# Cross attention with K made by seven products of halves and read back from DRAM, in place of scores from the context itself

## The chip, the core and the metric

One NeuronCore of a Trainium2 chip runs the whole program. The metric is the device time of one execution in microseconds (us), as a median of several runs. The engines are TensorE (PE; its weight loads are PEld), VectorE (DVE), ScalarE (ACT), GpSimd (POOL) and SyncE (SP), which here only issues DMAs.

## What is computed

The program is a small perceiver of two layers over x (8 batches of 64 tokens, width 512) with a context of 8 x 1601 rows of width 1024. The change lies in the cross attention of the second layer:

```python
B, N, DIM = (8, 2048, 512)
M, CTX = (128, 1024)
HEADS, DH = (16, 64)
...
q = _split_heads(jnp.einsum('bnd,df->bnf', x, Wq))
kv = jnp.einsum('bmc,cf->bmf', context, Wkv)
k, v = jnp.split(kv, 2, axis=-1)
...
k = jnp.concatenate((nk, k), axis=-2)
v = jnp.concatenate((nv, v), axis=-2)
q = q * scale
sim = jnp.einsum('bhid,bhjd->bhij', q, k)
attn = jax.nn.softmax(sim, axis=-1)
out = jnp.einsum('bhij,bhjd->bhid', attn, v)
```

All of it is f32. The kernel gets f32 accuracy from f16 products: a number is kept as a high half and a low half (what the high half leaves), and a product is the sum of three: high by high, high by low, low by high. So every operand is "split": ScalarE writes the high half, VectorE the low one (raw minus high).

## The kernel before

The program is a row of stages, each with its own instruction streams for the five engines and a barrier at its end; semaphores order the engines within a stage.

Through the first stages (names dp_, mi_, ms_, mo_, bn_ and cq_) TensorE also makes V = context x Wv (names vw_, class `ValueWork`) between the stages' own products, and writes it to DRAM (`vd`). The last 34 context tiles of V are made in stage cq by `QuadWork`, 17 quads. A quad takes two context tiles and both halves of the contraction and of the features, and makes the four blocks of the result by seven products of halves (Strassen's scheme in Winograd's form) instead of eight; GpSimd makes the sums of context blocks and splits four of the seven operands, VectorE splits three, ScalarE makes high halves, and VectorE adds the products up (line 677, `cq_held`) and splits the results (line 691, `vw_vst`). The products rotate over six PSUM banks.

Stage ca (`attend`) takes a step f for each of 64 pairs of heads (8 batches by 8 pairs; f = 8 b + p). It never makes K. In step f, `project` multiplies the K weights of the pair by the queries, laid out block-diagonally in `ca_q_diag` by GpSimd (24 products of 128 columns, lines 1820 to 1822), to the query in context space `ca_qw` (split by lines 1911 and 1964). `chunk` multiplies that by the context of the batch, `CUTS = [0, 448, 896, 1249, KEYS]`, with KEYS = 1602 (the null key is the last): 4 chunks x 8 parts of the contraction x 3, 96 products (lines 1841 to 1843). The context of the next batch is loaded tile by tile (`ca_stage`) and split (lines 1905, 1957) into a ring of three half batches. Then the softmax: VectorE takes the maxima of the two halves of the scores (line 1969) and the bias (1973), ScalarE the exponentials with their sums (1919), VectorE the reciprocal (1978, 1981), ScalarE the weights' high half (1928), VectorE the low half (1986). SP transposes both halves by DMA (`ca_turned`, line 1769), and two steps later `attend_to` multiplies them by V, which SP has loaded from `vd` (`ca_vals`). After four pairs VectorE copies the results out (`leave`, lines 1995 and 1997). The order on TensorE is written out:

```python
for f in range(NF + 2):
    if f < NF:
        chunk(f, 0)
    if f + 1 < NF:
        project(f + 1, 0)
    if f < NF:
        chunk(f, 1)
    if f >= 2:
        attend_to(f - 2)
```

and likewise on the other engines; each engine takes its instructions strictly in that order. During V's quads, the first half batch of the context is loaded and split for stage ca (`first_high`, `first_low`), and in the stage before eight K-weight items ("keyw") are split. After ca follows stage co (`project_out`).

## Time and profile before

| | |
|---|---|
| median of 3 runs | 3063.41 us (3062.07 to 3064.23) |
| the profiled execution | 3065.92 us, of which the span from first to last instruction is 3063.9 us |
| busy: TensorE, weight loads | 2838.0 us (93%), 1507.4 us (49%) |
| busy: VectorE, ScalarE, GpSimd | 1625.4 us (53%), 1041.0 us (34%), 248.5 us (8%) |
| mean granted TensorE clock | 0.967 of full |
| DMA | 343.00 MB, mean 112 GB/s; SP's queue 40.8% of 16 engines' span |

The busy time of an engine is the time in which at least one of its instructions ran. TensorE's products overlap, so the duration of one is longer than its distance to the next. Shares over the whole span are a mean over stages with different limits, which is why the rows below are from stretches of it.

### The profile page before, as it was taken

To read this page: it belongs to the slowest core of one execution; us is meant where nothing else is said; L and a number is where in the kernel's file an instruction comes from. 1 tells how busy PE (TensorE), PEld (TensorE's weight loads), DVE (VectorE), ACT (ScalarE), POOL (GpSimd) and SP (SyncE) were. 2 spreads that over 40 slices of the span, in tenths; PEclk is the share of its full clock that TensorE was granted. 3 is DMA by queue.
4 is the path that set the end of the run, shared out by engine and by line. 5 is a ranking of instruction groups with operands and counts; after the bars stand their busy time and mean duration, and the time that the engine had idled before them with its cause. 6 is when DMAs were issued, how large, how long until landed. Compare 5 with 4: busy or idle time off the path is not lost. (4 is left out here: it accounts for less than half of the span.)

```text
span 3063.9 us, 42939 instructions
## 1 busy us (share of the span) xinstructions
PE 2838.0 (93%) x17913; PEld 1507.4 (49%) x17921; DVE 1625.4 (53%) x1942; ACT 1041.0 (34%) x1621; POOL 248.5 (8%) x338
## 2 busy tenths in 40 slices
PE   6999999998989999989999999999999997786799
PEld 3334444443444444446665666666666664334453
DVE  5358999995565666643434343434343432367410
ACT  2254433431433443332333333333232321173210
POOL 1000000000000555500000000000000000100000
PEclk9999999999999999999999999999999998887899
DMA  5033334334323444345655565555555544100203
GB/s 203 24 108 103 96 108 129 94 97 163 126 83 126 146 128 139 113 129 116 146 117 143 117 149 116 149 115 150 115 150 114 130 86 104 59 7 22 110 21 131
DMA packets 487175, 343.00 MB, mean 112 GB/s; under 512 B 246884, under 2 KB 452005, under 8 KB 482759
## 3 DMA queue, kind: packets, MB, share of 16 engines
q1 hardware_dynamic: 486982, 340.26, 40.8%
q8 instruction: 142, 2.33, 0.3%
q14 instruction: 51, 0.41, 0.0%
HBM read 231.06 MB, written 54.62 MB: 93 GB/s over the span
## 5 line engine op out<-in xcount | busy, mean ns | idle before, releaser
L1841 PE MATMUL ca_p_s<-early_halves,ca_qw 128*128 128x448 f16 (+2 forms) x1408 | 466.7, 331 | 1.4 <-DVE ca_qw L1964 1.4
L1843 PE MATMUL ca_p_s<-early_halves,ca_qw 128*128 128x448 f16 (+2 forms) x1408 | 466.8, 332 | 0.0
L1842 PE MATMUL ca_p_s<-early_halves,ca_qw 128*128 128x448 f16 (+2 forms) x1408 | 466.8, 332 | 0.0
L1964 DVE TENSOR_TENSOR ca_qw<-ca_p_w,ca_qw 128x512 f16<-128x512 f32 x128 | 88.5, 691 | 508.3 <-ACT ca_qw L1911 508.3
L394 PE MATMUL vw_pv<-vw_wv,vw_ctx 128*128 128x512 f16 (+1 forms) x688 | 263.9, 384 | 36.6 <-PEq L74 15.3
L395 PE MATMUL vw_pv<-vw_wv,vw_ctx 128*128 128x512 f16 (+1 forms) x688 | 263.6, 383 | 0.0
L396 PE MATMUL vw_pv<-vw_wv,vw_ctx 128*128 128x512 f16 (+1 forms) x688 | 263.6, 383 | 0.0
L1911 ACT ACTIVATE ca_qw<-ca_p_w 128x512 f16<-128x512 f32 x128 | 76.4, 597 | 504.5 <-PE ca_p_w L1822 504.5
L1842 PE MATMUL ca_p_s<-ca_ctx,ca_qw 128*128 128x448 f16 (+2 forms) x640 | 216.2, 338 | 0.0
L1841 PE MATMUL ca_p_s<-ca_ctx,ca_qw 128*128 128x448 f16 (+2 forms) x640 | 216.1, 338 | 0.0
L1843 PE MATMUL ca_p_s<-ca_ctx,ca_qw 128*128 128x448 f16 (+2 forms) x640 | 216.1, 338 | 0.0
L1919 ACT ACTIVATE ca_probs<-ca_p_s,ca_small 128x896 f32<-128x896 f32 (+1 forms) x128 | 117.6, 924 | 219.5 <-DVE ca_small L1973 219.5
L1843 PEld LDWEIGHTS ca_p_s<-early_halves,ca_qw 128*128 128x128 f16 x1408 | 137.9, 98 | 99.1 <-issue 0.9
L1986 DVE SCALAR_TENSOR_TENSOR ca_parts<-ca_probs,ca_small,ca_parts 128x1602 f16<-128x1602 f32 x64 | 120.8, 1888 | 118.6 <-ACT ca_parts L1928 118.6
L1841 PEld LDWEIGHTS ca_p_s<-early_halves,ca_qw 128*128 128x128 f16 x1408 | 137.8, 98 | 90.5 <-DVE ca_qw L1964 1.7
L1842 PEld LDWEIGHTS ca_p_s<-early_halves,ca_qw 128*128 128x128 f16 x1408 | 137.8, 98 | 88.8 <-issue 0.9
L1248 ACT ACTIVATE work<-early_halves,mb_a_neg 128x252 f32<-128x252 f32 x256 | 104.7, 492 | 219.2 <-DVE ms_h L1281 215.5
L1969 DVE TENSOR_REDUCE ca_small<-ca_p_s 128x1 f32<-128x896 f32 (+1 forms) x128 | 126.5, 988 | 64.3 <-PE ca_p_s L1843 64.3
L394 PE MATMUL ms_pv<-vw_wv,vw_ctx 128*128 128x512 f16 x336 | 129.2, 385 | 16.8 <-DVE vw_ctx L370 8.6
L1281 DVE TENSOR_TENSOR_SCAN ms_h<-work,ms_h 128x2048 f32<-128x2048 f32 x32 | 141.3, 4417 | 0.0
L1806 POOL COPY ca_q_diag<-work 64x128 f16<-64x128 f16 x128 | 43.9, 343 | 1158.7 <-PE ca_p_s L1843 1154.8
L394 PEld LDWEIGHTS vw_pv<-vw_wv,vw_ctx 128*128 128x128 f16 (+1 forms) x688 | 67.7, 98 | 128.5 <-issue 27.5
(554 smaller groups left out, 5356.6 us busy)
## 6 DMA issues: line engine op xcount, KB each, us to landing
ca_stage<-in_ctx_t SPq DMA_DIRECT2D x97, 512.0 KB, 3.6
vd<-vw_vst SPq DMA_DIRECT2D x192, 256.0 KB, 2.3
ca_vals<-vd SPq DMA_DIRECT2D x64, 768.0 KB
vw_ring<-in_ctx_t SPq DMA_DIRECT2D x89, 512.0 KB, 3.8
ex_w_d<-in_w_d SPq DMA_DIRECT2D x8, 2048.0 KB, 7.2
vw_ring<-in_w_kv SPq DMA_DIRECT2D x16, 512.0 KB, 4.7
early_r<-state_rows SPq DMA_DIRECT2D x8, 1024.0 KB, 7.7
early_r<-in_w SPq DMA_DIRECT2D x2, 4096.0 KB, 14.3
```

What stands on the lines that cost most here:

```text
L394: self.nc.tensor.matmul(o, xh[:, c, 0:w], self.wv[0][:, c, f], start=(c == 0), stop=False)
L395: self.nc.tensor.matmul(o, xh[:, c, 0:w], self.wv[1][:, c, f], start=False, stop=False)
L396: last = self.nc.tensor.matmul(o, xl[:, c, 0:w], self.wv[0][:, c, f], start=False, stop=(c == CC - 1))
L1248: ins = nc.scalar.activation(da[q][:, m, :, 1:], steps, ACT.Exp, scale=a_neg[:, e, q * NQ + m:q * NQ + m + 1])
L1281: nc.vector.tensor_tensor_scan(flat, da[q].rearrange("p n b s -> p (n b s)"), flat, 0.0, ALU.mult, ALU.add).then_inc(scanned, 1)
L1841: nc.tensor.matmul(o, a[:, 0, c, :], x[:, 0, c, lo:hi], start=(c == 0), stop=False)
L1842: nc.tensor.matmul(o, a[:, 0, c, :], x[:, 1, c, lo:hi], start=False, stop=False)
L1843: last = nc.tensor.matmul(o, a[:, 1, c, :], x[:, 0, c, lo:hi], start=False, stop=(c == CC - 1))
L1919: nc.scalar.activation(probs[:, CUTS[2 * h]:CUTS[2 * h + 2]].rearrange("p (a n) -> p a n", a=2), scores(f, h), ACT.Exp, bias=nbias, scale= ...
L1964: nc.vector.tensor_tensor(qw[f % 2][:, 1, c, :], p_w[:, :].rearrange("p (c n) -> p c n", n=P), qw[f % 2][:, 0, c, :], ALU.subtract).then_i ...
L1969: nc.vector.tensor_reduce(peak[:, h:h + 1], scores(f, h), AX.XY, ALU.max).then_inc(peak_done, 1)
L1986: nc.vector.scalar_tensor_tensor(parts[:, 1, 0:KEYS], probs[:, :], rinv, parts[:, 0, 0:KEYS], ALU.mult, ALU.subtract).then_inc(wl_done, 1)
```

## The change

K is made after all. It is computed transposed (features on partitions, keys as columns), 32 quads of the context (8 batches by `KQ` = 4). A quad has two blocks of 201 keys (198 in a batch's last quad, the last place of which is the null key's) and two halves of the contraction and of the features, and takes seven products instead of eight. Each of the seven is made in two parts (h = 0, 1) of 2 x 24 products of 201 columns in one PSUM bank, so a quad has 14 parts (m = 0 to 13). Three banks rotate (`ca_p_k`); part m waits for the addition that has read part m - 3.

- GpSimd makes the four sums of context blocks (`sums_first`, `sums_second`), each of 804 columns, two of them building on the sum before. ScalarE makes all seven high halves, VectorE all seven low halves (`low`) and 14 additions (`add`, to `ca_held`); the four results are split (`out_high`, `out_low`) and stored by SP into `kd` in DRAM, in rows of 804 bytes.
- A quad takes two steps of the loops: the even one has parts 0 to 6, the odd one parts 7 to 13. The raw context of a quad is one pair of tiles with one buffer: the next load waits for the seventh low half.
- Scores of pair f come from 12 products with K loaded back from `kd` (`load_keys`). They run `BEHIND` = 9 steps behind the quads. So there are 73 steps on the engines: 9 with quads alone, 55 with both, 9 with attention alone. One set of four score banks replaces the ring of three pairs.
- The sums of K's weights (seven operands, in `tk`) are made and split in V's quads (`KeyWeights`: 8 steps, each over two quads; 7 splits and 4 sums of 256 columns a step), in place of `first_low` and the keyw items. Projections, the query splits and the context splits of stage ca are gone.

The core of the diff:

```diff
+KQ = 4
+KN = 201
+KN_LAST = KEYS // 2 - (KQ - 1) * KN
...
+            if i % 2:
+                self.keys.load(sp, i // 2 + 1)
...
+    def low_given(self, dve, s):
+        w11, w12, w21, w22 = self.quarters
+        for n in range(3):
+            self.low(dve, s, n)
+        dve.wait_ge(self.lo, 7 * s + 3)
+        self.nc.vector.tensor_tensor(w11, w12, w11, ALU.subtract).then_inc(self.made, 1)
+        dve.wait_ge(self.made, 4 * s + 1)
+        self.nc.vector.tensor_tensor(w12, w22, w12, ALU.subtract).then_inc(self.made, 1)
...
+    SLOTS = 9
+    STAGED = 3
+    BANKS = 3
+    QUADS = B * KQ
+    HALF = CC // 2
...
+    ADDS = [(1, 2, 1), (0, 1, 2), (2, 2, 3), (3, 0, 4), (1, 1, 4), (0, 0, 5), (1, 1, 6)]
+    ADD_AT = {(0, 0): 0, (0, 1): 1, (1, 0): 2, (1, 1): 3, (2, 0): 4, (2, 1): 5, (3, 0): 6, (4, 0): 7, (3, 1): 8, (4, 1): 9,
+              (5, 0): 10, (5, 1): 11, (6, 0): 12, (6, 1): 13}
+    AFTER = [None, 0, 0, 1, 1, 3, 4]
+    READ = [None, 0, 1, 2, 4, 5, 6]
...
+    def load(self, sp, i):
+        if i >= self.QUADS:
+            return
+        if i:
+            sp.wait_ge(self.op_lo, 7 * i)
+        for t in range(2):
+            sp.dma_start(self.raws[t][:, :, :].rearrange("p h n -> p (h n)"),
+                         self.io.ctx_k[i // KQ, i % KQ, t, :, :]).then_inc(self.ld[t], 16)
...
+    def sums_first(self, g, i):
+        if i >= self.QUADS:
+            return
+        s, (a, b) = self.sums, self.raws
+        for t in range(2):
+            g.wait_ge(self.ld[t], 16 * (i + 1))
+        if i:
+            g.wait_ge(self.op_lo, 7 * i)
+        g.tensor_tensor(s[:, 0, :], b[:, 0, :], b[:, 1, :], ALU.add).then_inc(self.s_made, 1)
+        g.wait_ge(self.s_made, 4 * i + 1)
+        g.tensor_tensor(s[:, 1, :], s[:, 0, :], a[:, 0, :], ALU.subtract).then_inc(self.s_made, 1)
+        g.wait_ge(self.s_made, 4 * i + 2)
+        g.tensor_tensor(b[:, 0, :], a[:, 0, :], b[:, 0, :], ALU.subtract).then_inc(self.s_made, 1)
+
+    def sums_second(self, g, i):
+        if i >= self.QUADS:
+            return
+        g.wait_ge(self.s_made, 4 * i + 3)
+        g.wait_ge(self.op_lo, 7 * i + 3)
+        g.tensor_tensor(self.sums[:, 0, :], self.raws[0][:, 1, :], self.sums[:, 1, :], ALU.subtract)\
+            .then_inc(self.s_made, 1)
...
+    def pe(self, pe, m):
+        i, r, h = m // 14, m % 14 // 2, m % 2
+        if h == 0:
+            pe.wait_ge(self.op_lo, 7 * i + r + 1)
+        if m >= self.BANKS:
+            j, q, g = (m - self.BANKS) // 14, (m - self.BANKS) % 14 // 2, (m - self.BANKS) % 2
+            if q:
+                pe.wait_ge(self.added, 14 * j + self.ADD_AT[self.READ[q], g] + 1)
+            else:
+                pe.wait_ge(self.copied, 2 * j + g + 1)
+        w, x, o, n = self.tk[r], self.slot(i, r), self.bank(m), self.wide(i)
+        for e in range(2):
+            f = slice((2 * h + e) * P, (2 * h + e + 1) * P)
+            for c in range(self.HALF):
+                k = slice(c * KN, c * KN + n)
+                self.nc.tensor.matmul(o[:, e, :], w[:, 0, c, f], x[:, 0, k], start=(c == 0), stop=False)
+                self.nc.tensor.matmul(o[:, e, :], w[:, 0, c, f], x[:, 1, k], start=False, stop=False)
+                last = self.nc.tensor.matmul(o[:, e, :], w[:, 1, c, f], x[:, 0, k], start=False, stop=(c == self.HALF - 1))
+        last.then_inc(self.prod, 1)
...
+    def out(self, sp, i, k):
+        sp.wait_ge(self.out_lo, 4 * i + k + 1)
+        t, g = self.OUTS[k]
+        n = 4 * i + k
+        sp.dma_start(self.kd[i // KQ, i % KQ, t, g * GP:(g + 1) * GP, :, :].rearrange("c p n -> p c n"),
+                     self.staged[n % self.STAGED].rearrange("p c l n -> p c (l n)")).then_inc(self.k_out[n % self.STAGED], 16)
+
+    def landed(self, sp, b):
+        last = 4 * KQ * (b + 1)
+        for s in range(self.STAGED):
...
+        PARTS = 2 * kw.QUADS
+        BEHIND = 2 * KQ + 1
+        STEPS = NF + BEHIND
...
+            def load_keys(f):
+                b, p = divmod(f, PAIRS)
+                if p == 0:
+                    kw.landed(sp, b)
+                if f >= 2:
+                    sp.wait_ge(scored, 2 * (f - 1))
...
+            for t in range(STEPS):
+                f, (i, later) = t - BEHIND, divmod(t, 2)
+                if t and not later:
+                    kw.load(sp, i + 1)
+                if 0 <= f + 1 < NF:
+                    load_keys(f + 1)
+                if t < PARTS and later:
+                    kw.out(sp, i, 0)
+                if f >= 0:
+                    turn(f, 0)
+                    turn(f, 1)
+                if t < PARTS and later:
+                    kw.out(sp, i, 1)
+                    kw.out(sp, i, 2)
+                if 2 <= f + 1 < NF:
+                    load_values(f + 1)
+                if t < PARTS and later:
+                    kw.out(sp, i, 3)
...
+                for n in range(KQ):
+                    w = KN if n < KQ - 1 else KN_LAST
+                    o = p_s[:, n * BANK:n * BANK + 2 * w].rearrange("p (a n) -> p a n", n=w)
+                    nc.tensor.matmul(o, q[:, 0, :], x[:, 2 * n:2 * n + 2, 0, 0:w], start=True, stop=False)
+                    nc.tensor.matmul(o, q[:, 0, :], x[:, 2 * n:2 * n + 2, 1, 0:w], start=False, stop=False)
+                    last = nc.tensor.matmul(o, q[:, 1, :], x[:, 2 * n:2 * n + 2, 0, 0:w], start=False, stop=True)
+                    if n >= KQ - 2:
+                        last.then_inc(scored, 1)
...
-            project(0, 0)
-            project(0, 1)
-            for f in range(NF + 2):
-                if f < NF:
-                    chunk(f, 0)
-                if f + 1 < NF:
-                    project(f + 1, 0)
-                if f < NF:
-                    chunk(f, 1)
-                if f >= 2:
-                    attend_to(f - 2)
-                if f < NF:
-                    chunk(f, 2)
-                if f + 1 < NF:
-                    project(f + 1, 1)
-                if f < NF:
-                    chunk(f, 3)
...
+            for t in range(STEPS + 1):
+                f = t - BEHIND
+                if 0 <= f < NF:
+                    score(f)
+                if t < PARTS:
+                    for n in range(3):
+                        kw.pe(pe, 7 * t + n)
+                if f >= 1:
+                    attend_to(f - 1)
+                if t < PARTS:
+                    for n in range(3, 7):
+                        kw.pe(pe, 7 * t + n)
...
+            for t in range(STEPS + 1):
+                f, (i, later) = t - BEHIND, divmod(t, 2)
+                quad = t < PARTS
+                if 0 <= f < NF:
+                    peak_of(f)
+                if quad and later:
+                    kw.add(dve, i, 2, 1)
+                if 0 <= f < NF:
+                    inverse(f)
+                if quad and later:
+                    kw.add(dve, i, 3, 0)
+                    kw.add(dve, i, 4, 0)
+                if 0 <= f < NF:
+                    weights_low(f)
+                if quad and not later:
+                    kw.add(dve, i, 0, 0)
+                    kw.add(dve, i, 0, 1)
+                    kw.low(dve, i + 1, 0)
+                    kw.low(dve, i + 1, 1)
+                    kw.add(dve, i, 1, 0)
+                    kw.low(dve, i + 1, 2)
+                    kw.add(dve, i, 1, 1)
+                    kw.add(dve, i, 2, 0)
+                elif quad:
+                    kw.add(dve, i, 3, 1)
+                    kw.add(dve, i, 4, 1)
+                    kw.out_low(dve, i, 0)
+                    kw.low(dve, i + 1, 3)
+                    kw.low(dve, i + 1, 4)
+                    kw.out_low(dve, i, 1)
+                    kw.low(dve, i + 1, 5)
+                    kw.add(dve, i, 5, 0)
+                    kw.add(dve, i, 5, 1)
+                    kw.out_low(dve, i, 2)
+                    kw.low(dve, i + 1, 6)
+                    kw.add(dve, i, 6, 0)
+                    kw.add(dve, i, 6, 1)
+                    kw.out_low(dve, i, 3)
+                if f >= 1 and (f - 1) % GP == GP - 1:
+                    leave((f - 1) // GP)
```

Two places in the order of instructions. VectorE in stage ca, before: one whole step (lines as above; x2 means twice in a row).

```order
L1969 TENSOR_REDUCE ca_small<-ca_p_s 128x1
L1973 TENSOR_SCALAR ca_small<-ca_small 128x1
L1964 TENSOR_TENSOR ca_qw<-ca_p_w,ca_qw 128x512
L1978 TENSOR_SCALAR ca_small<-ca_small 128x1
L1981 RECIPROCAL ca_small<-ca_small 128x1
L1986 SCALAR_TENSOR_TENSOR ca_parts<-ca_probs,ca_small,ca_parts 128x1602
L1969 TENSOR_REDUCE ca_small<-ca_p_s 128x1
L1964 TENSOR_TENSOR ca_qw<-ca_p_w,ca_qw 128x512
```

VectorE in stage ca, after: the end of an odd step, from additions 3 and 4 (half 0) on. Line 1880 is `add`, 1900 `out_low`, 1834 `low` (its operand tiles lie in `early_region` and `ca_slot`), 2169 the low half of the weights.

```order
L1880 TENSOR_TENSOR ca_held<-ca_p_k,ca_held 128x402 x2
L2169 SCALAR_TENSOR_TENSOR ca_parts<-ca_probs,ca_small,ca_parts 128x1602
L1880 TENSOR_TENSOR ca_held<-ca_p_k,ca_held 128x402 x2
L1900 TENSOR_TENSOR ca_k_out<-ca_held,ca_k_out 128x4x201
L1834 TENSOR_TENSOR early_region<-early_region 128x804 x2
L1900 TENSOR_TENSOR ca_k_out<-ca_held,ca_k_out 128x4x201
L1834 TENSOR_TENSOR early_region<-ca_sums,early_region 128x804
L1880 TENSOR_TENSOR ca_held<-ca_p_k,ca_held 128x402 x2
L1900 TENSOR_TENSOR ca_k_out<-ca_held,ca_k_out 128x4x201
L1834 TENSOR_TENSOR early_region<-early_region 128x804
L1880 TENSOR_TENSOR ca_held<-ca_p_k,ca_held 128x402 x2
L1900 TENSOR_TENSOR ca_k_out<-ca_held,ca_k_out 128x4x201
```

The query splits are gone from VectorE's step; eight splits and eight additions stand behind the weights in the odd step, and additions 5 come after five of the splits.

SP's DMAs in stage ca, before: one step (a context tile, two transposes, the values).

```order
L1750 DMA ca_stage<-in_ctx_t 128x1024
L1769 DMA_TRANSPOSE ca_turned<-ca_parts 128x13x128 x2
L1757 DMA ca_vals<-vd 128x12x256
L1759 DMA ca_vals<-vd 65x256
```

SP's DMAs in stage ca, after: from the last store of a quad on, the rest of the even step.

```order
L1907 DMA kd<-ca_k_out 128x4x402
L1778 DMA early_region<-in_ctx_k 128x1608 x2
L1962 DMA ca_keys<-kd 128x7x402
L1964 DMA ca_keys<-kd 128x2x197
L1984 DMA_TRANSPOSE ca_turned<-ca_parts 128x13x128 x2
L1973 DMA ca_vals<-vd 128x12x256
L1975 DMA ca_vals<-vd 65x256
```

The context load of the next quad (line 1778) stands on SP behind the quad's last store, and the keys' load, the transposes and the values stand behind it.

## Rows read from the trace of the kernel before

**Rows 1.** The page's head: the span.

```profile
span 3063.9 us, 42939 instructions
```

**Rows 2.** Windows: span; busy us and count by engine; PEclk, DMA share, GB/s.

```profile
1040.00:1300.00 260.00, 260.00 (x1206) 117.84 (x1205) 172.29 (x207) 102.93 (x180) 146.60 (x115) 1.00 0.44 130
...
1343.00:2560.00 1217.00, 1205.39 (x10950) 751.55 (x10949) 478.52 (x628) 388.84 (x536) 42.79 (x124) 1.00 0.55 126
2560.00:2586.00 26.00, 12.80 (x211) 9.30 (x208) 5.82 (x9) 4.10 (x6) 0.00 (x0) 0.77 0.39 83
```

**Rows 3.** Timeline of TensorE: start, duration (us), instruction, idle before.

```profile
1331.45 0.29 PE L1820 MATMUL ca_p_w<-ca_q_diag,early_r 128*128 128x128 f16 x1 [6.66 <-POOL ca_q_diag L1806]
```

**Rows 4.** Timeline of VectorE at the end of stage ca.

```profile
2574.68 1.89 DVE L1986 SCALAR_TENSOR_TENSOR ca_parts<-ca_probs,ca_small,ca_parts 128x1602 f16<-128x1602 f32 x1 [1.85 <-ACT ca_parts L1928]
2582.97 0.42 DVE L1995 TENSOR_SCALAR work<-ca_p_o 128x256 f32<-128x256 f32 x1 [6.40 <-PE ca_p_o L1873]
```

**Rows 5.** Timeline of VectorE, the same instruction in two steps.

```profile
2495.32 0.21 DVE L1973 TENSOR_SCALAR ca_small<-ca_small 128x1 f32<-128x1 f32 x1
...
2514.38 0.21 DVE L1973 TENSOR_SCALAR ca_small<-ca_small 128x1 f32<-128x1 f32 x1
```

**Rows 6.** Timeline of TensorE in a steady step (rows of one form between left out).

```profile
1349.90 0.31 PE L1843 MATMUL ca_p_s<-early_halves,ca_qw 128*128 128x353 f16 x1
...
1353.20 0.22 PE L1820 MATMUL ca_p_w<-ca_q_diag,early_r 128*128 128x128 f16 x1
...
1353.87 0.31 PE L1841 MATMUL ca_p_s<-early_halves,ca_qw 128*128 128x352 f16 x1
```

**Rows 7.** Groups by form, VectorE, 1500 to 2400 us: busy us, mean ns.

```profile
L1986 DVE SCALAR_TENSOR_TENSOR ca_parts<-ca_probs,ca_small,ca_parts 128x1602 f16<-128x1602 f32 x47 | 88.7, 1888 | 87.2 <-ACT ca_parts L1928 87.2
L1964 DVE TENSOR_TENSOR ca_qw<-ca_p_w,ca_qw 128x512 f16<-128x512 f32 x94 | 65.0, 691 | 375.7 <-ACT ca_qw L1911 375.7
L1957 DVE TENSOR_TENSOR early_halves<-ca_stage,early_halves 128x1024 f16<-128x1024 f32 x43 | 52.5, 1231 | 17.2 <-ACT early_halves L1905 17.1
L1969 DVE TENSOR_REDUCE ca_small<-ca_p_s 128x1 f32<-128x896 f32 x47 | 50.9, 1083 | 0.0
L1969 DVE TENSOR_REDUCE ca_small<-ca_p_s 128x1 f32<-128x706 f32 x48 | 42.8, 892 | 33.6 <-PE ca_p_s L1843 33.6
```

**Rows 8.** Groups in V's quads, 1040 to 1300 us, VectorE and GpSimd.

```profile
L677 DVE TENSOR_TENSOR cq_held<-cq_p_q,cq_held 128x512 f32<-128x512 f32 x66 | 45.3, 686 | 23.3 <-PE cq_p_q L751 22.7 <-issue 0.3
...
L631 POOL TENSOR_TENSOR cq_sums<-vw_ring,cq_sums 128x512 f32<-128x512 f32 x14 | 18.2, 1300 | 1.1
```

**Rows 9.** Groups by form, ScalarE, 1500 to 2400 us.

```profile
L1928 ACT ACTIVATE ca_parts<-ca_probs,ca_small 128x1602 f16<-128x1602 f32 x47 | 76.7, 1631 | 54.8 <-DVE ca_small L1981 54.8
...
L1919 ACT ACTIVATE ca_probs<-ca_p_s,ca_small 128x896 f32<-128x896 f32 x48 | 48.3, 1007 | 152.5 <-DVE ca_small L1973 152.5
L1905 ACT ACTIVATE early_halves<-ca_stage 128x1024 f16<-128x1024 f32 x43 | 44.6, 1049 | 13.1 <-DMA ca_stage<-in_ctx_t 13.1
L1919 ACT ACTIVATE ca_probs<-ca_p_s,ca_small 128x706 f32<-128x706 f32 x48 | 40.3, 840 | 0.0
...
L1919 ACT ACTIVATION_READ_ACCUMULATOR ca_probs<-ca_p_s,ca_small 128x1 f32 x95 | 18.6, 196 | 0.0
```

**Rows 10.** DMA view: values, 2562.2:2568.2; transposes, 2574:2583; issues, 1343:2560 (us to landing).

```profile
q1 hardware_dynamic: 1654, 0.82, 49.4%
...
q1 hardware_dynamic: 3392, 0.85, 50.8%
...
ca_stage<-in_ctx_t SPq DMA_DIRECT2D x91, 512.0 KB, 3.6
ca_turned<-ca_parts SPq DMA_TRANSPOSE x126, 4.0
```

**Rows 11.** Timelines of GpSimd and VectorE in V's quads.

```profile
1230.25 1.26 POOL L631 TENSOR_TENSOR cq_sums<-vw_ring,cq_sums 128x512 f32<-128x512 f32 x1
...
1230.48 1.58 DVE L691 TENSOR_TENSOR vw_vst<-cq_held,vw_vst 128x512 f16<-128x512 f32 x1
```

530 lines of the change are left out of this document (289 added, 241 removed).

## Prediction

> **What bounds the kernel now.** I read the page's head first, then the table of windows, then the timeline of TensorE inside the stage that is changed. The profiled execution spans 3063.9 us [rows 1]. The cross attention (names with ca_) takes the longest stretch of it: in 1343 to 2560 us TensorE is busy 1205.4 of 1217 us at full clock, VectorE 478.5, ScalarE 388.8, GpSimd 42.8, and the DMA engines carry a share of 0.55 [rows 2]. The reader is to see there one full engine and four with room. The stage's first product starts at 1331.45, 6.66 us after the one before it [rows 3], and its last VectorE instruction starts at 2582.97 and takes 0.42, a second like it follows [rows 4]: from 1324.8 to 2583.9 it costs 1259 us. In a steady step the same small instruction comes at 2495.32 and at 2514.38 [rows 5], so that one of the 64 steps lasts 19.06 us. In the V products before (1040 to 1300) TensorE is busy 260 of 260 us, VectorE 172 [rows 2].
>
> How fast TensorE really is shows in the distance of starts, not in durations: from 1349.90 to 1353.20 there are 22 products of 353 columns, 0.150 us each, and from 1353.20 to 1353.87 twelve of 128 columns, 0.056 each, every one with weights of its own [rows 6]. That is N columns at 2.4 GHz plus some 2.5 ns, and it puts a product of 201 columns at 0.086 us, of 402 at 0.170, of 448 at 0.189.
>
> **The change on TensorE.** Removed from each step: 24 projections (24 x 0.056 = 1.3 us) and 96 score products (24 x (0.189 x 2 + 0.150 x 2) = 16.3). What is left of the 19.06 is about 1.3 us for the product with V. Added: 12 score products of 402 or 396 columns (2.0 us), and for each of 32 quads of the context 7 x 48 products of 201 columns, 336 x 0.086 = 28.9 us. A quad spans two steps, so a full pair of steps is 28.9 + 2 x (2.0 + 1.3) = 35.5 us against 38.1 before. Over the stage that is 32 x 28.9 + 64 x 3.3 = 1136 us, where before it was 64 x 19.06 = 1220: were TensorE still the bound everywhere, 84 us would go. I don't think it stays the bound, in three places.
>
> **VectorE's work in a pair of steps.** Two sizes of a row give the slope: a split of 1024 takes 1.23 us [rows 7] and an addition from PSUM of 512 takes 0.69 [rows 8], about 1.05 ns an element; a split of 804 is 1.0 us and an addition of 402 is 0.57. The softmax instructions of a step are the maxima (1.08 for 896, 0.89 for 706, so 1.4 + 0.6 for 1206 and 396), small ones of 0.2 (three), and the low half of the weights, 1.89 [rows 7]: 4.5 us. A pair: 7 + 4 splits (11), 14 additions (8), 2 x 4.5: 28 us, against some 15.5 us for a pair now (2 x 4.5, four query splits of 0.7, 3.25 context splits of 1.2). That fits into 35.5 us only if VectorE never waits long, and it runs a fixed order through waits.
>
> **The loop that sets the pace.** TensorE has three banks for K products. The fourteenth product of a quad waits for the addition that reads the eleventh (add 5, half 0), which stands in VectorE's order behind two output splits and three operand splits. And the next context load waits on SP behind the store of the quad's last output, since it stands behind it, while the raw tiles have one buffer. So the loop runs, from the end of add (5, 0):
> 1. add (5, 1) 0.5; ScalarE's copy 0.9 and VectorE's split 1.0 of output 2; operand split 1.0; two additions 1.0; copy and split of output 3, 1.9: together 6.2 us (ScalarE's 804 elements by 1.05 us for 1024 [rows 9]; instructions that follow without a wait overlap by some 0.07).
> 2. SP issues the store and then the two loads, 1.65 MB. Half a megabyte lands in 3.6 us [rows 10]. The other 1.13 MB at the rate of a values load (0.82 MB in 49.4% of 6 us = 2.96 us of all engines [rows 10], so 277 GB/s) add 4.1; behind a store and the values another 1 to 2. Bounds 6.5 and 11; I take 8.9 with the issue.
> 3. GpSimd must make two sums one after the other before split 1. For it only 512 elements are measured, 1.30 us [rows 8]; in proportion 2.0. Two are 4.0, copy 0.9, split 1.0. GpSimd and VectorE hinder each other: a GpSimd addition runs from 1230.25 to 1231.51, and a VectorE split of 512 (0.69 when alone, as the query split of that size [rows 7]) started at 1230.48 takes 1.58, until 0.55 us after the other's end [rows 11]. I charge 0.8 here and 0.5 for split 2. With additions (1, 0), (1, 1), (2, 0) this is 6.7 + 3.0 us.
> 4. The odd step: maxima and bias 2.15, exponentials 1.95 (1.01 for 896, 0.84 for 706 and 0.2 for each read [rows 9]), sum and reciprocal 0.4, high weights 1.7, low weights 1.85, two additions, five splits and add (5, 0), 6.2: 14.3 us.
> The sum is 6.2 + 8.9 + 9.7 + 14.3 = 39.1, with 0.4 for the results' copies 39.5 us a pair, 4 more than TensorE asks and 1.4 more than the pair lasts now. Bounds: TensorE's 35.5, and 43 with the slow landing and full waits between GpSimd and VectorE. I take 39.5, since every link but the landing has a row.
>
> **Head and tail.** K of a whole batch must be in DRAM before its scores, so they run nine steps behind. In the head (4.5 quads) only K is made. The first product waits for a load, a copy and a split: 12 us after the last V product instead of 6.7. The first quad makes its seven splits in one run before an addition is served, and only then is the second load let go: 44 us. Then the same loop without softmax: 34.5 us a quad (6.2 + 8.9 + 9.7 + 8, and some waits for products) against 28.9 on TensorE. In the tail nine steps have scores and no K products, and a chain paces them: high weights 1.7, low weights 1.9, the transposing DMA's landing 4.0 [rows 10], then the next high weights may write the same tile: 7.6 us at the least. But the queue also carries two transposes (50.8% of 9 us = 4.6 us [rows 10]), the values 3.0 and the keys, as many bytes as the values, 3.0: 10.6 us a step. Before, such a step's end is seen once: the low weights start at 2574.68, take 1.89, and the last product with V is read at 2582.97 [rows 4]. Nine steps of 10.6, TensorE's last product at the lower clock (0.77 of full in 2560 to 2586 [rows 2]), and two copies: 101 us, at least 73.
>
> **The sum.** 12 + 44 + 3.5 x 34.5 + 27.5 x 39.5 + 101 = 1364 us against 1259: 105 more. What moves into the V products is small for TensorE: 88 instructions of 256 elements on VectorE (0.42 each, 37 us), less seven and eight splits of 1024 (18 us), spread over 16 quads in which VectorE has 88 of 260 us free [rows 2], behind products that have six banks. I cost it at nothing; if that cover were gone it would be some 15 us. 3063.9 + 105 = 3169 of span. The profiled run took 3065.9 us, 2.0 more than its span, while the median is 3063.4: I say 3170 us.
>
> **DMA as the cover that may go.** A pair would ask for 9.2 (transposes) + 6 (values) + 6 (keys read) + 6 (keys written) + 6.8 (context: the share 0.55 of 1217 us, less 61 values loads and 63 pairs of transposes, leaves 2.15 us for each of 91 loads of half a megabyte [rows 2, 10]) = 34 of 39.5 us, where now it is 21 of 38. The prices of keys are by bytes from the values' row, since no row has packets of 804 bytes. The Trainium skill (DMA: Bandwidth & Descriptors, How a descriptor splits into AXI transactions) says that a descriptor that doesn't start on 256 bytes also fetches what lies before its start. No run here shows it yet; estimated by that page, rows of 804 bytes would cost some 15% more a byte than rows of 512, about 2 us a pair, which could add up to 55 us if all of it came into the landing.
>
> **Rivals.**
> - Loads land early and GpSimd's sums fall between the splits: pair 37, head 33.5, tail 95: 12 + 41 + 117 + 1018 + 95 = 1283, 3090 us. For it: 0.5 MB lands in 3.6 us. Against it: the queue is fuller by half. Chance 0.20 (3070 to 3130).
> - DMA becomes the bound: packets of 804 bytes are dear or the landing grows under load, pair 43, head 37, tail 115: 12 + 46 + 130 + 1183 + 115 = 1486, 3290 us; half of that effect is 3230. Chance 0.13.
> - The other side: TensorE stays the bound. Pair 36, head 31, tail 88: 12 + 40 + 109 + 990 + 88 = 1239, 3045 us. This needs the context load to land within 5.5 us and no hindrance by GpSimd; it decides from a pair of about 35.7 us with my head and tail, 37.7 with the best of both. For it: TensorE saves 84 us. Against it: [rows 11] and step 3 of the loop. Chance 0.09, with 0.03 for no change.
> - The forecast, pair 38.5 to 41: chance 0.55, own range 3130 to 3215.
>
> **How the numbers follow.** Faster by over 0.2% (6 us, about what a measurement of this kernel can tell) 0.09, within it 0.03, slower 0.88. The range 3075 to 3230 leaves out the faster cases (about 0.1) and the upper part of the DMA rival and of the slack of the forecast (about 0.1).
>
> **What would show it.** In the profile of the changed kernel: pairs of K products' quads 38 to 41 us apart in the middle; TensorE idle before the fourteenth product with the addition to ca_held as releaser, some 3 us a quad; GpSimd waiting for the load and VectorE for GpSimd's sums; a granted clock still near full in the middle; nine steps of about 10 us at the end with the transpose as releaser. The prediction is wrong if VectorE's additions are ready before each product wants its bank, if the raw tiles land in under 6 us, or if the keys' loads are what TensorE waits for.

## The result, and the profile of the changed kernel

The changed kernel takes 3274.28 us (median of 4 runs, 3272.61 to 3275.81), the kernel before 3063.82 us beside it: 1.0684 times as long, 95% interval 1.0666 to 1.0703. The forecast said slower, 3170 us in 3075 to 3230. The side was right, the size was not: 210 us more, not 106, and outside the range.

The page's head, and the windows that answer to [rows 2] (span; busy us and count of TensorE, weight loads, VectorE, ScalarE, GpSimd; granted clock, DMA share, GB/s):

```profile
span 3272.3 us, 52729 instructions
```

```profile
1040.00:1300.00 260.00, 235.16 (x1032) 101.67 (x1030) 178.35 (x234) 94.22 (x186) 127.81 (x97) 0.95 0.36 111
1343.00:2560.00 1217.00, 1083.94 (x12938) 988.55 (x12935) 771.30 (x1082) 478.85 (x654) 290.87 (x237) 0.96 0.77 183
1600.00:2600.00 1000.00, 908.76 (x11336) 835.48 (x11334) 657.55 (x933) 415.83 (x562) 228.97 (x198) 0.98 0.87 203
2690.00:2780.00 90.00, 43.95 (x460) 24.38 (x460) 35.70 (x50) 24.91 (x35) 3.47 (x12) 0.64 0.95 213
```

The first line is the surprise. In V's quads TensorE was busy 260 of 260 us; now it is busy 235, at a mean clock of 0.95. The third is the steady middle: TensorE 91%, no engine full. The last is the tail, the DMA engines at 0.95 and TensorE half idle at 0.64.

The borders, from the timelines of TensorE and ScalarE (start, duration). The first row is the last V product, which ends at 1372.3 (before, it ended at 1324.8), the second K's first product, the next two the first copies of K quads 4 and 31, the last K's last product:

```profile
1371.95 0.38 PE L715 MATMUL vw_pv<-cq_t,vw_ctx 128*128 128x512 f16 x1
1387.07 0.35 PE L1855 MATMUL ca_p_k<-early_region,early_r 128*128 128x201 f16 x1 [14.74 <-DVE early_region L1834]
...
1543.66 0.49 ACT L1867 ACTIVATE ca_held<-ca_p_k 128x402 f32<-128x402 f32 x1
...
2649.42 0.50 ACT L1867 ACTIVATE ca_held<-ca_p_k 128x396 f32<-128x396 f32 x1 [2.54 <-PE ca_p_k L1857]
...
2680.58 0.25 PE L1857 MATMUL ca_p_k<-ca_slot,early_region 128*128 128x198 f16 x1
```

A pair of steps in the middle is (2649.42 - 1543.66) / 27 = 40.95 us. The stage's last VectorE instruction, which answers to the second of [rows 4], ends at 2793.5; what comes behind it takes as long as before (477.5 us from the next stage's first copy, 478.4 before).

**The new stall in V's quads.** Timelines of SP, ScalarE, VectorE and TensorE around one of six stalls:

```profile
1195.25 1.04 SPq L806 DMA_DIRECT2D early_region<-in_w_kv  x2
...
1199.87 0.72 ACT L817 ACTIVATE early_r<-early_region 128x256 f16<-128x256 f32 x2 [5.29 <-DMA early_region<-in_w_kv]
...
1201.52 0.69 DVE L631 TENSOR_TENSOR cq_parts<-vw_ring,cq_parts 128x512 f16<-128x512 f32 x1 [6.70 <-ACT cq_parts L625]
1202.12 0.68 DVE L655 TENSOR_TENSOR cq_held<-cq_p_q,cq_held 128x512 f32<-128x512 f32 x1
...
1202.95 0.58 PE L713 MATMUL cq_p_q<-vw_wv,cq_parts 128*128 128x512 f16 x1 [4.04 <-DVE cq_held L655]
1203.34 0.63 PE L714 MATMUL cq_p_q<-vw_wv,cq_parts 128*128 128x512 f16 x1
...
1208.16 0.38 PE L714 MATMUL vw_pv<-early_region,vw_ctx 128*128 128x512 f16 x1
```

Read it from the top. SP loads the next piece of the key weights at 1195.25, behind the stores of the odd quad. ScalarE's copy of them (high_given) stands at the start of the even quad, and waits 5.29 us for the landing. Behind it on ScalarE stand the context's copies; VectorE waits 6.70 us for one of these, with its additions behind it; TensorE has no free bank and idles 4.04 us. And then it pays again: its next products start 0.43 us apart, which is the lower of the clock's levels (1.2 GHz), up to 1207.95, and 0.22 apart after that. The same stall ends at 1116, 1159, 1246, 1289 and 1333: idle time 25 us in these six, 56 products at the lower clock 11.5 us more. From the first to the last product of V's quads (L713; L749 in the kernel before) it takes 353.7 us instead of 307.6.

**The loop in the middle**, one round, by VectorE, SP and GpSimd. It answers to the prediction's steps 1 to 3:

```profile
1952.00 1.00 DVE L1900 TENSOR_TENSOR ca_k_out<-ca_held,ca_k_out 128x804 f16<-128x804 f32 x1 [0.94 <-ACT ca_k_out L1896]
...
1949.61 0.67 SPq L1973 DMA_DIRECT2D ca_vals<-vd  x1
1950.33 0.99 SPq L1975 DMA_DIRECT2D ca_vals<-vd  x1
1953.03 0.37 SPq L1907 DMA_DIRECT2D kd<-ca_k_out  x1
1953.44 1.60 SPq L1778 DMA_DIRECT2D early_region<-in_ctx_k  x2
...
1964.94 1.89 POOL L1805 TENSOR_TENSOR ca_sums<-early_region 128x804 f32<-128x804 f32 x1 [30.56 <-DMA early_region<-in_ctx_k]
1966.91 1.88 POOL L1807 TENSOR_TENSOR ca_sums<-ca_sums,early_region 128x804 f32<-128x804 f32 x1
...
1969.80 1.80 DVE L1834 TENSOR_TENSOR ca_slot<-ca_sums,ca_slot 128x804 f16<-128x804 f32 x1 [6.08 <-ACT ca_slot L1826]
1971.53 0.56 DVE L1880 TENSOR_TENSOR ca_held<-ca_p_k,ca_held 128x402 f32<-128x402 f32 x1
...
1987.55 1.05 DVE L1880 TENSOR_TENSOR ca_held<-ca_p_k,ca_held 128x402 f32<-128x402 f32 x2
```

From the last output split's end (1953.0) to GpSimd's first sum it takes 11.9 us; from there through two sums, ScalarE's copy, split 1 (1.80 us where alone it takes 0.99) and four instructions 9.0, to 1973.9; the odd step up to addition (5, 0) ends at 1988.1, 14.2 us on; the next round's output split ends 6.3 us later. The forecast had 8.9, 9.7, 14.3 and 6.2. The landing alone is off: over the rounds of 1600 to 2540 us the sum starts 10.9 us (median) after the load's issue. Over 25 rounds the four links are 11.4, 9.1, 14.2 and 6.3 us in the mean, 40.9 together.

What it costs TensorE stands in its waits in 1600:2440 (who waited for whom: us, times, longest) and in one round:

```profile
PE ca_p_k L1855 <- DVE ca_held L1880: 72.6, 42, 2.7
```

```profile
1888.20 0.26 PE L1855 MATMUL ca_p_k<-ca_slot,early_r 128*128 128x201 f16 x1 [2.46 <-DVE ca_held L1880]
...
1904.23 0.26 PE L1855 MATMUL ca_p_k<-early_region 128*128 128x201 f16 x1 [1.92 <-DVE ca_held L1880]
```

The first row is the quad's eighth part (m = 7): it waits for addition (1, 0), which stands on VectorE behind split 1, and that waits for the sum. The second is the fourteenth, which waits for addition (5, 0). In the mean of 24 quads TensorE idles 2.3 us before the eighth and 1.3 before the fourteenth, and before no other part of K.

**The tail**: VectorE's low weights, one in each step:

```profile
2706.57 1.89 DVE L2169 SCALAR_TENSOR_TENSOR ca_parts<-ca_probs,ca_small,ca_parts 128x1602 f16<-128x1602 f32 x1 [1.83 <-ACT ca_parts L2118]
...
2715.86 1.89 DVE L2169 SCALAR_TENSOR_TENSOR ca_parts<-ca_probs,ca_small,ca_parts 128x1602 f16<-128x1602 f32 x1 [1.84 <-ACT ca_parts L2118]
...
2729.78 1.89 DVE L2169 SCALAR_TENSOR_TENSOR ca_parts<-ca_probs,ca_small,ca_parts 128x1602 f16<-128x1602 f32 x1 [1.84 <-ACT ca_parts L2118]
```

Behind a first step of 16.9 us (2689.7 to 2706.6), steps of about 9 and 14 us take turns, 11.1 in the mean of the seven up to 2784.3. TensorE's waits in 2690:2780 name the keys:

```profile
PE ca_p_s L2061 <- DMA ca_keys<-kd: 27.3, 5, 12.8
PE ca_p_s L2061 <- issue: 15.6, 3, 5.6
PE ca_p_o L2081 <- DMA ca_turned<-ca_parts: 7.6, 3, 2.9
```

The longest of them belongs to the first step, and is another thing than the order on the queue:

```profile
2683.49 0.42 SPq L1907 DMA_DIRECT2D kd<-ca_k_out  x1
2691.45 0.36 SPq L1962 DMA_DIRECT2D ca_keys<-kd  x1
...
2696.98 0.50 PE L2061 MATMUL ca_p_s<-ca_keys,ca_q_diag 128*128 128x402 f16 x1 [12.85 <-DMA ca_keys<-kd]
```

The first pair of the last batch needs the last stores of K in DRAM (`landed`), and then its keys loaded back: SP issues the last store at 2683.49 and the keys 8 us later, and TensorE stands still for 12.85 us.

### The profile page after: what moved, and what is told of

Its sections match the earlier page's. It is cut to its first block and busy times, and to the rows that moved or that the text cites. A ratio compares the mean times of both kernels' runs of the same rounds, so it can differ in the third digit from the quotient of the medians.

```text
span 3272.3 us, 52729 instructions
## 1 busy us (share of the span) xinstructions
PE 2848.7 (87%) x21569; PEld 1854.7 (57%) x21569; DVE 2037.4 (62%) x2592; ACT 1194.4 (37%) x1853; POOL 512.6 (16%) x469
## 5 line engine op out<-in xcount | busy, mean ns | idle before, releaser
L1855 PE MATMUL ca_p_k<-early_region,early_r 128*128 128x201 f16 (+1 forms) x1376 | 353.4, 257 | 67.6 <-DVE ca_held L1880 49.2
L1857 PE MATMUL ca_p_k<-early_region,early_r 128*128 128x201 f16 (+1 forms) x1376 | 351.1, 255 | 0.0
L1856 PE MATMUL ca_p_k<-early_region,early_r 128*128 128x201 f16 (+1 forms) x1376 | 351.0, 255 | 0.0
L1855 PE MATMUL ca_p_k<-early_region 128*128 128x201 f16 (+1 forms) x1024 | 260.3, 254 | 25.8 <-DVE ca_held L1880 25.7
L1880 DVE TENSOR_TENSOR ca_held<-ca_p_k,ca_held 128x402 f32<-128x402 f32 (+1 forms) x448 | 238.9, 566 | 43.6 <-PE ca_p_k L1857 43.2
L1856 PE MATMUL ca_p_k<-early_region 128*128 128x201 f16 (+1 forms) x1024 | 258.0, 252 | 0.0
L1857 PE MATMUL ca_p_k<-early_region 128*128 128x201 f16 (+1 forms) x1024 | 257.6, 252 | 0.0
L1896 ACT ACTIVATE ca_k_out<-ca_held 128x804 f16<-128x804 f32 (+1 forms) x128 | 111.8, 873 | 248.3 <-DVE ca_held L1880 248.3
L2109 ACT ACTIVATE ca_probs<-ca_p_s,ca_small 128x1206 f32<-128x1206 f32 (+1 forms) x128 | 117.6, 925 | 225.9 <-DVE ca_small L2154 225.4
L1855 PE MATMUL ca_p_k<-ca_slot,early_r 128*128 128x201 f16 (+1 forms) x672 | 171.9, 256 | 31.4 <-DVE ca_held L1880 31.3
L1303 ACT ACTIVATE work<-early_region,mb_a_neg 128x252 f32<-128x252 f32 x256 | 104.7, 492 | 220.7 <-DVE ms_h L1336 217.1
L1855 PEld LDWEIGHTS ca_p_k<-early_region,early_r 128*128 128x128 f16 x1376 | 136.5, 99 | 80.0 <-DVE ca_held L1880 56.8
L1857 PE MATMUL ca_p_k<-ca_slot,early_r 128*128 128x201 f16 (+1 forms) x672 | 170.9, 254 | 0.0
L1856 PE MATMUL ca_p_k<-ca_slot,early_r 128*128 128x201 f16 (+1 forms) x672 | 170.8, 254 | 0.0
L1900 DVE TENSOR_TENSOR ca_k_out<-ca_held,ca_k_out 128x804 f16<-128x804 f32 (+1 forms) x128 | 126.4, 988 | 60.3 <-ACT ca_k_out L1896 60.3
L1834 DVE TENSOR_TENSOR early_region<-ca_sums,early_region 128x804 f16<-128x804 f32 x64 | 80.2, 1254 | 109.8 <-ACT early_region L1826 109.8
```

The lines of the kernel that those rows point to most:

```text
L1303: ins = nc.scalar.activation(da[q][:, m, :, 1:], steps, ACT.Exp, scale=a_neg[:, e, q * NQ + m:q * NQ + m + 1])
L1855: self.nc.tensor.matmul(o[:, e, :], w[:, 0, c, f], x[:, 0, k], start=(c == 0), stop=False)
L1856: self.nc.tensor.matmul(o[:, e, :], w[:, 0, c, f], x[:, 1, k], start=False, stop=False)
L1857: last = self.nc.tensor.matmul(o[:, e, :], w[:, 1, c, f], x[:, 0, k], start=False, stop=(c == self.HALF - 1))
L1880: self.nc.vector.tensor_tensor(self.part(out, h, w), self.bank(m), self.part(other, h, w), ALU.add)\
L1896: self.nc.scalar.activation(self.out_place(i, k, 0), self.result(i, k), ACT.Copy).then_inc(self.out_hi, 1)
```

## The experiments

All twelve start from the changed kernel (3274.28 us). The kernel before measured 3061.5 to 3065.1 us beside them.

| run | edit | median us | ratio to the kernel before (95%) |
|---|---|---|---|
| e1 | key weights' first copies later | 3221.97 | 1.052 (1.0504 to 1.0536) |
| e2 | additions ahead of splits | 3211.8 | 1.049 (1.0474 to 1.0506) |
| e3 | context load ahead of values | 3184.49 | 1.0402 (1.0385 to 1.042) |
| e4 | rows of K every 1024 bytes | 3243.83 | 1.059 (1.0574 to 1.0606) |
| e5 | e1 to e4 together | 3085.94 | 1.0075 (1.0051 to 1.0098) |
| e6 | no sums by GpSimd | 3103.98, one run | |
| e7 | 11 of 13 tiles of V not loaded | 3236.41, one run | |
| e8 | tail's keys issued early | 3252.07 | 1.0613 (1.0596 to 1.0631) |
| e9 | e5 and e8 | 3080.14 | 1.0062 (1.0044 to 1.008) |
| e10 | e9 and e6 | 3059.85, one run | |
| e11 | rows every 1056 bytes | 3237.9 | 1.0579 (1.0547 to 1.0612) |
| e12 | rows every 1028 bytes | 3261.55 | 1.0655 (1.0628 to 1.0683) |

**e1: the wait in V's quads.** Both engines' order; ScalarE's is

```
             self.keep(act, i)
-            if step and not later:
-                keys.high_given(act, s)
...
             if step and later:
                 keys.high(act, s, 6)
+            elif step:
+                keys.high_given(act, s)
```

> Moves the key weights' three first copies (ScalarE) and their splits and two differences (VectorE) from the start of each even V quad to its end; no work is taken out, no load is moved. Theory A (the trace of the changed kernel): at the start of each even quad ScalarE waits some 5.3 us for the key weights to land, with the next context splits queued behind it, VectorE waits behind ScalarE and TensorE behind VectorE's additions, about 4.1 us of idle and 2.5 us at the lower clock after it, six times. Then the six stalls of about 4 us go, the last V product ends within 6 us of the kernel before (1324.8 us) and the time falls by 38 to 47 us, to 3227 to 3236 us. Theory B (the 37 us of added VectorE work itself, and its meeting GpSimd, fill VectorE): the stalls stay about as long in sum, in other places, and the time is 3260 to 3275 us.

Measured: 52 us less. TensorE's only wait in 1040:1320, and the window that answers to [rows 2]:

```profile
PE cq_p_q L713 <- DVE cq_held L655: 1.9, 3, 0.8
```

```profile
1040.00:1300.00 260.00, 258.87 (x1200) 116.58 (x1199) 216.20 (x274) 109.47 (x217) 147.52 (x113) 1.00 0.42 128
```

VectorE does all its added work (216 us where [rows 2] have 172) and TensorE is full again, at full clock. V's quads take 310.0 us, 2.4 more than before the change. So the work was nearly free, as forecast, and the wait for a landing cost 44 us (353.7 less 310.0). The other 8 of the 52, which put the time past the expected 38 to 47, lie behind V's quads, where nothing was edited: 5.5 in stage ca and 1.5 behind it. Such differences occur: over the thirteen traces of changed kernels, what comes behind the stage takes 472.4 to 480.9 us, though no edit reaches it.

**e2: VectorE's order in K's quads.**

```
                     kw.low(dve, i + 1, 0)
-                    kw.low(dve, i + 1, 1)
                     kw.add(dve, i, 1, 0)
-                    kw.low(dve, i + 1, 2)
                     kw.add(dve, i, 1, 1)
+                    kw.low(dve, i + 1, 1)
                     kw.add(dve, i, 2, 0)
+                    kw.low(dve, i + 1, 2)
```

> In the even step of a K quad VectorE makes additions (1,0) and (1,1) ahead of the operand split 1 that waits for GpSimd's second sum, and addition (2,0) ahead of split 2; nothing else is changed. Theory A (the pace is VectorE's fixed order: additions that TensorE's banks need stand behind splits that wait for the load and the sums): pairs of steps shorten from 41 to 39 to 40 us, quads of the head by 3 to 4 us, together 35 to 65 us less: 3210 to 3240 us. Theory B (the DMA queue, 86% busy in the middle, sets the pace): pairs stay within 0.4 us of 41 and only the head gains, 3255 to 3270 us.

Measured: 62 us less, theory A. The first copies of quads 0 to 4 lie 121 us apart instead of 144, pairs in the middle 39.7 instead of 40.95 (1.25 x 27 = 34 us). That is 57 of the 62. TensorE's wait before the eighth part is gone (2.3 us before), while the one before the fourteenth grows from 1.3 to 2.4.

**e3: SP's order.**

```
                     kw.out(sp, i, 2)
+                    kw.load(sp, i + 2)
                 if 2 <= f + 1 < NF:
                     load_values(f + 1)
```

with the load at the head of the next pair taken out.

> SP issues the next quad's two context loads right behind the stores of outputs 1 and 2, before the values' load and before the wait for output 3; nothing else is changed. The load is let go some 3 us earlier and has 0.8 MB of values less ahead of it. Theory A (the load's landing is a link of the loop, as forecast): GpSimd's first sum starts 4 to 6 us earlier against the splits before it, pairs 38.5 to 40 us, quads of the head 3 us less: 3195 to 3245 us. Theory B (the queue itself is the bound): the landing takes as much longer as it starts earlier, or the keys and values come late instead, TensorE waits for them and the time stays above 3260 us.

Measured: 90 us less, more than any other edit and 10.5 us beyond the range of theory A. In the trace, which is of the fastest of four executions (3172.26 us), pairs are 38.2 us, and GpSimd's sum starts 9.5 us after the issue instead of 10.9. From the last output split to the sum it takes 6.6 us in the mean instead of 11.4; of these 4.8 us the next link, up to addition (2, 0), takes 2.1 back. The queue is fuller for it (share 0.92 in 1600:2540), yet TensorE waits for neither values nor keys: theory B falls. The step of the forecast that this is (a load stands behind a store on SP) was named, and undoing it gives back 2.8 us a pair. The edit moves the load ahead of the store and of the values at once; no run tells the two apart.

**e4, e11, e12: where rows of K start.** The tensor's last dimension changes, from 402 to 512, 528 and 514 elements of 2 bytes, and stores and loads take the first 402 of it; as much is moved.

> K's rows in DRAM start every 1024 bytes instead of every 804; as many bytes are written and read. Theory A (a row that doesn't start on a boundary costs more): the queue's busy share in the middle falls by 3 to 6 points, keys land in under 5.8 us instead of 6.2, tail steps shorten by 0.5 us and the time falls by 10 to 35 us. Theory B (rows cost by bytes and number alone): the queue's share, the landings and the time stay the same, 3268 to 3280 us.

> As the run with rows of K on 1024 bytes, but the rows start every 1056 bytes: the same gap behind each row, seven of eight starts off a boundary of 256 bytes. Theory A (where a row starts is what costs): the queue's share in the middle and the time are those of rows of 804 bytes, 3266 to 3280 us. Theory B (the gap or the spread over memory is what helped, not the start): 3238 to 3252 us, as with 1024 bytes.

> As before with rows of K every 1028 bytes: a gap of 224 bytes behind each row, but starts on multiples of 4 bytes alone, as with 804. Rows of 1056 bytes start on multiples of 32 and were as good as rows of 1024. Theory A (starts on 32 bytes are what helps): the time is that of rows of 804 bytes, 3266 to 3280 us, stores land after 4.8 to 5.0 us. Theory B (the gap helps, wherever the row starts): 3236 to 3252 us, stores land after 4.0 us.

The queue and K's stores in 1600:2550 (packets, MB, share; KB each, us to landing), in the changed kernel, with 1024, 1056 and 1028 bytes:

```profile
q1 hardware_dynamic: 343301, 191.99, 87.1%
...
kd<-ca_k_out SPq DMA_DIRECT2D x92, 402.0 KB, 5.2
```

```profile
q1 hardware_dynamic: 350526, 195.84, 83.3%
...
kd<-ca_k_out SPq DMA_DIRECT2D x96, 402.0 KB, 4.1
```

```profile
q1 hardware_dynamic: 351390, 197.00, 83.4%
...
kd<-ca_k_out SPq DMA_DIRECT2D x96, 402.0 KB, 4.0
```

```profile
q1 hardware_dynamic: 342805, 191.35, 86.6%
...
kd<-ca_k_out SPq DMA_DIRECT2D x93, 402.0 KB, 5.6
```

A packet and a byte are as many in each; with 1024 bytes the queue works 0.833 x 40.07 = 33.4 us a pair, with 804 bytes 0.871 x 40.95 = 35.7. The 2.3 us are about the 2 that the prediction took from the Trainium skill (DMA: Bandwidth & Descriptors, How a descriptor splits into AXI transactions), but its reason doesn't hold here: by it a row that starts off 256 bytes costs more when it is read, and rows every 1056 bytes, seven of eight of them off 256, are as good as rows every 1024. Rows every 1028 bytes have nearly the same gap and are as slow in stores (5.6 us), queue and pairs (40.8) as 804. The rows thus point to starts on 32 bytes, and not to the gap; 8 and 16 were not tried.

The gain is in the stores: the keys' loads land after 6.2 us in three of the four runs and 6.3 in the other, where e4's theory A had under 5.8, and the tail is as long as before. The two loads of context behind a store gain too: 9.7 us to landing with 804 bytes, 8.3 with 1024, 8.0 with 1056. With 1028 it is 8.7, which neither theory of e12 had, and its time, 3262 us, lies between their ranges; 5 of its 13 us under the changed kernel come before K's first product. So that starts on 32 bytes are the whole cause is likely and not shown. Of the 30 us of e4, 24 are in the 27 pairs of the middle (40.07 instead of 40.95), and 6 lie behind the stage.

**e6, e7: what the loop is made of.** In e6 no sum is made and every operand is split from a quarter of the context; in e7 `n = FULL if f < 2 else 1` of the 12 full tiles of V are loaded. The piece of 65 rows is loaded as before, so 11 of 13 tiles keep old data, not the 12 of the expectation.

> GpSimd makes no sums: all seven operands are split straight from the context's quarters, so what the products get is not the sums (work left out: 4 GpSimd additions of 804 columns a quad); copies, splits, products, loads, stores stay. Theory A (the two sums in a row, 3.8 us, the copy behind them, and GpSimd and VectorE hindering each other are links of the loop): pairs 36 to 37.5 us instead of 41, quads of the head 31 to 32.5 instead of 37, the time 3110 to 3160 us. Theory B (the landing hides them, or the queue is the bound): pairs stay at 40 or more, above 3240 us.

> From the third step on only the first 128 of the 1601 rows of V are loaded in each step (12 of 13 tiles keep old data): some 2.7 us of the queue's work less a step, 5.5 a pair. Theory A (the loop through the load's landing and VectorE's order sets the pair, the queue only lengthens the landing): pairs 39 to 40.3 us instead of 41; the tail, where the queue is over 92% busy, falls from 12.4 to 10 us a step; the time 3205 to 3245 us. Theory B (the queue is the bound of the middle): pairs fall by the whole 5.5 us to TensorE's 35.5 to 36, the time is below 3140 us.

```profile
1600.00:2440.00 840.00, 838.39 (x10779) 780.97 (x10772) 612.32 (x884) 394.50 (x533) 39.69 (x184) 1.00 0.98 229
```

```profile
1600.00:2600.00 1000.00, 934.95 (x11623) 857.71 (x11621) 693.03 (x953) 422.18 (x576) 266.70 (x204) 0.98 0.73 173
```

Without sums (first line) pairs are 36.2 us and TensorE is busy 838 of 840: it is the bound, though the DMA engines are at 0.98. The time is 6 us below the expected range, the pairs are inside theirs. With 14 points less on the queue (second line) pairs are still 39.95 us. The queue is not the bound of the middle; it lengthens one link, by 2.3 us (9.2 instead of 11.4 from the last output split to the sum, which starts 8.6 us after the issue), and 1 us of it reaches the pair. GpSimd's sums are worth 4.7 us a pair, near the 4.0 + 0.8 + 0.5 of the forecast's step 3; it is a lower bound, since TensorE is full without them. Of e7's 38 us the middle gives 27 and the tail 13, while the head loses 2: in the tail its seven steps behind the first fall from 11.1 to 9.8 us, with the DMA engines at 0.79 there (2663:2744).

**e5, e8, e9, e10: together, and the tail.** e8 is

```
-                if 0 <= f + 1 < NF:
+                if 0 <= f + 1 < NF and t <= PARTS:
                     load_keys(f + 1)
+                if PARTS <= t and f + 2 < NF:
+                    load_keys(f + 2)
```

> The four edits before together: key weights' first copies and splits at the end of even V quads, additions ahead of splits 1 and 2, context loads ahead of the values, rows of K every 1024 bytes. Theory A (they remove different waits): their savings of 52, 62, 90 and 30 us overlap only where two shorten the same loop, the head at TensorE's 29 us a quad, pairs 37 to 38, the tail still about 110: 3040 to 3085 us. Theory B (in the middle the queue, at 33 to 35 us of work a pair and with waits for its order, becomes the bound at once): pairs stay at 38 or more and the time is 3090 to 3130 us.

> In the last nine steps SP issues the keys of the step after next right when their buffer is free, ahead of the two transposes and the values; the same bytes move. Theory A (the tail's steps of 12.4 us come from SP's order: the keys are issued behind the values and TensorE waits for them): steps fall to about 9 to 10 us, 3245 to 3255 us. Theory B (the queue, 93% busy, is full whatever the order): steps of 11.6 or more, the time falls by less than 10 us, 3264 to 3276 us.

> The four edits together and the keys of the tail issued early. Theory A (the tail's order of issues is its own wait, beside the others): tail steps from 12.4 to 10 us, 10 to 22 us less than with the four edits: 3062 to 3078 us, no gain over the kernel before (its own median here about 3064). Theory B (with rows of K on 1024 bytes the tail's order no longer matters): 3082 to 3090 us.

> The five edits and no sums on GpSimd (operands split straight from the context's quarters, work left out): what is left when VectorE and GpSimd leave TensorE alone in the middle. If TensorE is the bound of the middle already with the five edits, pairs stay at 36 to 36.5 us and the time within 25 us of the run with five edits: 3040 to 3070 us. If waits for the sums still cost 1 us or more a pair, it falls under 3040 us.

In e8's tail the low weights come evenly:

```profile
2719.39 1.89 DVE L2171 SCALAR_TENSOR_TENSOR ca_parts<-ca_probs,ca_small,ca_parts 128x1602 f16<-128x1602 f32 x1 [2.30 <-ACT ca_parts L2120]
...
2729.33 1.89 DVE L2171 SCALAR_TENSOR_TENSOR ca_parts<-ca_probs,ca_small,ca_parts 128x1602 f16<-128x1602 f32 x1 [1.84 <-ACT ca_parts L2120]
...
2739.29 1.89 DVE L2171 SCALAR_TENSOR_TENSOR ca_parts<-ca_probs,ca_small,ca_parts 128x1602 f16<-128x1602 f32 x1 [1.83 <-ACT ca_parts L2120]
```

The seven steps behind the first take 9.8 us in the mean instead of 11.1: 10 us of the 22 gained are here (from K's last product to the stage's end 103 us instead of 113). The rest, 5 us before K's first product and 6 behind the stage, lies where nothing was edited, and is spread between executions. TensorE's waits now go to the transposes; of those for the keys the first one, 11.9 us for K's last stores and the load behind them, is the only one left (window 2690:2770):

```profile
PE ca_p_o L2083 <- DMA ca_turned<-ca_parts: 29.7, 8, 5.6
PE ca_p_s L2063 <- DMA ca_keys<-kd: 11.9, 1, 11.9
```

The queue's packets fill the whole tail here (share 1.07 in 2690:2770), but in e7 the same 9.8 us came with 0.79. So the queue's work is not all that is left; TensorE takes the next scores behind a product with V that waits for the transposes, and I think that this chain over two steps is the other part. No run takes it apart.

The four edits of e5 save 188 us together, where alone they save 235; the time is 1 us above the range of theory A, and pairs are 36.95 us, less than theory B's 38. What is missing of the sum is near what pairs can't gain any more, for TensorE needs 36.2. In e9 (window of the middle, and its first copies of quads 4 and 31):

```profile
1600.00:2440.00 840.00, 825.84 (x10534) 765.97 (x10532) 636.39 (x863) 383.45 (x522) 257.46 (x180) 1.00 0.91 226
```

```profile
1465.71 0.49 ACT L1867 ACTIVATE ca_held<-ca_p_k 128x402 f32<-128x402 f32 x1
...
2462.58 0.50 ACT L1867 ACTIVATE ca_held<-ca_p_k 128x396 f32<-128x396 f32 x1 [1.25 <-PE ca_p_k L1857]
```

a pair takes 36.9 us, and 36.6 without sums (e10), whose time of 3060 us is inside its expected 3040 to 3070: the sums cost some 0.35 us a pair now. e9's gain of 6 us over e5 missed its expectation of 10 to 22; in the traces the tail gains 8 (103 us instead of 111), and e9's executions spread over 12 us (3077.5 to 3089.6). It remains 0.6% slower than the kernel before, with an interval clear of 1: no version that does the whole work is faster than the kernel before.

## Why the prediction had the side right and the size wrong

By its own sum of 1364 us, the parts of the 105 us that were missing:

- **V's quads, costed at nothing: +47.** The first step that failed, and the largest. I asked whether VectorE had time for 88 more instructions, and it has (e1). I did not ask it of the wait that came with them: K's loop was walked through wait by wait, V's quads were not: `high_given` waits for a DMA with the context's copies queued behind it. My bound of 15 us was of the work, not of that wait. The clock made a stall of 4.1 us one of about 6.
- **Pairs 39.5: measured 40.95, with the middle +36.** The mechanism was right: additions behind splits, splits behind sums, sums behind the landing, the load behind a store; e2, e3 and e6 each shorten it as they should. The mis-sized term is the landing (step 2): 8.9 us, measured 11.9 in the round shown and 11.4 in the mean, beyond my bound of 11; the other links are right within 0.6. What I had priced at 1 to 2 us stands in SP's rows: 0.8 MB of values issued 3.8 us ahead of the load, and K's stores, which land after 5.2 us each.
- **Start 12: measured 14.7. Head 44 + 3 x 34.5: some 7 more.** Sizes. The head's quads run the same loop; for the start no run shows the reason.
- **Tail 101: measured 112.7.** Two terms. The first of the nine steps takes 17 us, not 10.6, since the last stores of K and the load of the keys behind them stand in series before it; the forecast had no term for that, and no edit here takes it away. The seven behind it take 11.1, not 10.6: keys stand behind values behind the transposes on SP, and e8's order makes them 9.8. So the queue's work is about as forecast, but not a floor of the step: in e8 it is 1.07 x 9.8 = 10.5 us by the packets' times, in steps of 9.8.
- **The DMA rival** gave 3290 us. That DMA is the bound of the middle is not what happened: in e6 pairs of 36.2 us ran with the DMA engines at 0.98. But its other half, a landing that grows under load, is: half of its effect is a stage of 1425 us (halfway from 1364 to 1486), and 1421 were measured (V's last product to the stage's end). That the total came near 3290 is luck, for the other 47 us lie in V's quads, where it had nothing. **TensorE's side** is right as a floor: I had 35.5 us a pair, 36.2 was measured. Its break-even "with the best of both" is a slip: by that rival's own start, head and tail, (1259 - 12 - 40 - 109 - 88) / 27.5 is 36.7 us, not 37.7. e9, with 36.9, is slower than the kernel before.
- **The signs.** Pairs of 38 to 41 us, the granted clock (0.98 in 1600:2600), VectorE's wait for the sums and TensorE's 3.6 us of waits for additions came as said, but 2.3 of the 3.6 lie before the eighth part, which the forecast doesn't name. The tail's releaser was to be the transpose; there TensorE waits for the keys, 27 us in 90, and that was one of the signs of being wrong. In the middle (1600:2440) TensorE waits for no DMA.

Where did TensorE's 84 us go? In e9, with most waits out, K's products take 1157 us from first to last where the 64 steps took 1220, so 63 are there. Against them stand the tail, 103 us of nine steps with little on TensorE, where before the stage ended 15 us after its last score product, and a start 7 us longer: 14 + 1157 + 103 is 1274 us, against 1259. A stage that must finish K in DRAM before its first scores pays that at the end, and there e8's order of the queue gave back 10 us.
